# Three attentions with a unit's weighted sums in three parts between the next unit's transposes, and sixteen products ahead of each

## The reference

```python
# layer 0: q = layernorm(x), k = v = ctx, 16 heads of 8
energy = where(mask == 0, -1e20, einsum('nqhd,nkhd->nhqk', q, k))
out = einsum('nhqk,nkhd->nqhd', softmax(energy / sqrt(128)), v)
x = x + (out @ W_out + b_out)
# layer 2: two attention maps over the same values
attn1 = softmax(q1 @ k1.T * SCALE); attn2 = softmax(q2 @ k2.T * SCALE)
y = (attn1 - lambda_full * attn2) @ v1
x = x + (rms_norm(y) * norm_w @ proj_w.T + proj_b)
# layer 3: rotated q and k, a bias by position, a gate over the result
attended = (softmax(q @ k.T * SCALE + bias) @ v) @ Wout.T + b_out
gate = sigmoid(attended @ Wgate.T + b_gate)
x = x + (gate * attended + (1 - gate) * q_input_before_norm)
```

## Time and profile before

| | |
|---|---|
| runs | 1301.16 us median (1288.03 to 1305.8, 3 runs) |
| profiled execution | 1308.73 us, its span 1306.9 us |
| mean granted clock of TensorE | 0.814 |
| busy, share of the span | PE 82%, PEld 75%, DVE 51%, ACT 39%, POOL 30% |
| busy, us | PE 1077.4, DVE 670.0, ACT 513.0, POOL 397.4 |

### The profile page before, as it was taken

The page is one execution under the profiler, slowest core; times in us unless marked ns, Lnnn a source line. Parts: engine busy times, 40 slices in busy tenths (PEclk is TensorE's granted clock), DMA queues, the critical chain, the costliest instruction groups (busy, mean ns, idle before and its releaser), DMA issues. The chain is left out here.

```text
span 1306.9 us, 19893 instructions
## 1 busy us (share of the span) xinstructions
PE 1077.4 (82%) x7374; PEld 976.3 (75%) x7374; DVE 670.0 (51%) x1808; ACT 513.0 (39%) x987; POOL 397.4 (30%) x396
## 2 busy tenths in 40 slices
PE   3899999999988999889989762989169987359992
PEld 2888889999977899768888662888148877358882
DVE  7788511111257343667778643343567655444443
ACT  1443434444433334444444321655224323045552
POOL 4333300010013002300010054446634335545552
PEclk9866589999995899968788765999667656579996
DMA  9999800000000000000000013654200000155553
GB/s 324 170 172 170 156 1 1 1 1 1 1 1 1 1 1 1 1 1 1 1 1 2 1 33 115 177 172 147 65 1 1 1 1 20 36 168 174 174 165 97
DMA packets 70574, 83.52 MB, mean 64 GB/s; under 512 B 5297, under 2 KB 57528, under 8 KB 70352
## 3 DMA queue, kind: packets, MB, share of 16 engines
q1 hardware_dynamic: 64336, 71.71, 24.1%
q0 software_dynamic: 4992, 8.45, 1.9%
q10 hardware_dynamic: 1152, 2.10, 0.4%
HBM read 51.88 MB, written 32.18 MB: 64 GB/s over the span
## 5 line engine op out<-in xcount | busy, mean ns | idle before, releaser
L2167 ACT ACTIVATE hT<-PS,par 128x512 f32<-128x512 f32 x200 | 137.3, 689 | 186.4 <-PE PS L2115 184.9
L2207 DVE SCALAR_TENSOR_TENSOR X<-PS,wts,X 128x128 f32<-128x128 f32 x272 | 76.6, 344 | 231.5 <-PE PS L2127 231.5
L837 PEld LDWEIGHTS PS<-vblk,hT 128*128 128x128 f32 (+1 forms) x1152 | 175.1, 239 | 0.0
L1050 ACT ACTIVATE hT<-PS 128x512 f32<-128x512 f32 (+1 forms) x192 | 91.4, 490 | 205.0 <-PE PS L820 195.3
L837 PE MATMUL PS<-vblk,hT 128*128 128x27 f32 (+2 forms) x1152 | 170.3, 301 | 0.0
L820 PE MATMUL PS<-par,score 128*128 128x128 f32 (+1 forms) x640 | 135.8, 365 | 15.3 <-ACT score L1030 8.1
L820 PEld LDWEIGHTS PS<-par,score 128*128 128x128 f32 (+1 forms) x640 | 106.4, 190 | 25.2 <-issue 13.9
L2127 PEld LDWEIGHTS PS<-regA,hT 128*128 128x128 f32 x1024 | 119.2, 192 | 2.8
L2127 PE MATMUL PS<-regA,hT 128*128 128x128 f32 x1024 | 119.5, 275 | 0.0
L1097 POOL TENSOR_TENSOR score<-score,mx 128x1232 f32<-128x1232 f32 x32 | 72.0, 2249 | 121.7 <-DVE mx L922 121.7
L1878 PE MATMUL PS<-q_up,halves 128*112 128x256 f32 (+1 forms) x276 | 87.9, 318 | 16.1 <-DVE hT L1990 8.8
(11 more groups left out here) (301 smaller groups left out, 2108.9 us busy)
## 6 DMA issues: line engine op xcount, KB each, us to landing
regA<-L3f_w SPq DMA_DIRECT2D x23, 704.0 KB
regB<-L2f_w SPq DMA_DIRECT2D x23, 578.0 KB
L2f_sorted_x<-empty_row SPq DMA_DIRECT2D x8, 1161.0 KB, 21.9
L3f_sorted_x<-empty_row SPq DMA_DIRECT2D x8, 1161.0 KB, 22.1
regA<-L0f_w SPq DMA_DIRECT2D x4, 768.0 KB, 15.9
regA<-L2f_sorted_x SPq DMA_DIRECT2D x23, 129.0 KB, 3.7
regB<-L3f_sorted_x SPq DMA_DIRECT2D x23, 129.0 KB, 4.0
par<-params SPq DMA_DIRECT2D x1, 2386.0 KB, 12.2
```

Of the source, the lines that this page charges most:

```text
L837: last = nc.tensor.matmul(PS[:, 6, h0 * VW:(h0 + nh) * VW], pT, vblk[0:w, b, 3 * j * VW:(3 * j + nh) * VW], start=False, stop=j == NBLK - 1)
L1050: nc.scalar.activation(hT[:, u % 2, i, 0:full], PS[:, bank, 0:full], ACT.Copy)\
L2167: nc.scalar.activation(hT[:, n % 2, k, :], PS[:, i % 4, :], c["act"], bias=pc(f"{tag}_b1")[:, col:col + 1]).then_inc(h_ready.sem, 1)
```

## The change

On TensorE the weighted sums of unit u - 1 are made in iteration u, in three parts that follow the three parts of unit u's transposes; `lag` grows by one. Sixteen products of the identity with itself, which nobody reads, stand between `scores(1)` and the loop. The copies of the turned output (and of the turned attended rows in L3x) go from VectorE to ScalarE. The addition to X (or the gate's) moves into the next unit's `maxima`, between its two operations, and a new signal `att_ready` (after the bias is added) takes the place of `x_done` and `attT` as what the next output transpose waits for. ScalarE copies the first part of a unit's turned blocks before the exponentials of the next unit and the others behind them. Steps of the next norm and of the router start one to three tiles later. The diff, cut to its core:

```diff
-            lag = 1 if tag == "L3x" else 2
+            lag = 2 if tag == "L3x" else 3
...
-                def weighted(u):
+                def weighted(u, i):
                     b = tile_of(u) // TG
-                    if u:
+                    if i == 0 and u:
                         pe.wait_ge(o_used.sem, o_used.at(u))
-                    if tag == "L3x" and u >= 2:
+                    if i == 0 and tag == "L3x" and u >= 2:
                         pe.wait_ge(g_in.sem, g_in.at(u - 1))
-                    for j, (h0, nh, w) in enumerate(BLOCKS):
-                        if j % 4 == 0:
-                            pe.wait_ge(pT_ready.sem, pT_ready.at(3 * u + j // 4 + 1))
+                    pe.wait_ge(pT_ready.sem, pT_ready.at(3 * u + i + 1))
+                    for j in groups[i]:
+                        h0, nh, w = BLOCKS[j]
...
-                        free = aT_ready if tag == "L3x" else x_done
-                        pe.wait_ge(free.sem, free.at(t))
+                        pe.wait_ge(att_ready.sem, att_ready.at(t))
...
                 scores(0)
                 scores(1)
+
+                for _ in range(16):
+                    nc.tensor.matmul(PS[:, 6, 0:P], ident, ident, start=True, stop=True)
                 for u in range(units + lag):
...
                     if 0 < u < units:
-                        transposes(u, (0, 1))
+                        transposes(u, (0,))
+                    if 0 < u <= units:
+                        weighted(u - 1, 0)
+                    if 0 < u < units:
+                        transposes(u, (1,))
                     if done is not None:
                         out_project(done)
+                    if 0 < u <= units:
+                        weighted(u - 1, 1)
...
                     if 0 < u < units:
                         transposes(u, (2,))
+                    if 0 < u <= units:
+                        weighted(u - 1, 2)
...
-                    if u < units:
-                        weighted(u)
...
-                def maxima(u):
+                def maxima(u, between=None):
...
+                    if between:
+                        between()
                     v.wait_ge(scores_used.sem, scores_used.at(u + 1))
                     nc.vector.tensor_reduce(m, dst, AX.X, ALU.max).then_inc(to_shift.sem, 1)
...
                 def finish(t):
                     v.wait_ge(y_psum.sem, y_psum.at(t + 1))
...
+                    att = gdiff[:, t % 2, :] if tag == "L3x" else fin[:, 2 + t % 2, :]
+                    nc.vector.tensor_tensor(att, PS[:, 7, P:2 * P], pc(f"{tag}_bo"), ALU.add).then_inc(att_ready.sem, 1)
+
+                def add_attended(t):
+                    v.wait_ge(att_ready.sem, att_ready.at(t + 1))
+                    nc.vector.tensor_tensor(X[:, t, :], X[:, t, :], fin[:, 2 + t % 2, :], ALU.add).then_inc(x_done.sem, 1)
...
+                    before_last = u - lag - 1
+                    add_to_x = None
+                    if sets == 1 and before_last >= 0:
+                        def add_to_x(t=before_last):
+                            (gate_out if tag == "L3x" else add_attended)(t)
                     if u + 2 < units:
-                        maxima(u + 2)
+                        maxima(u + 2, add_to_x)
...
-                    if u < units:
-                        normalise(u)
+                    if 0 < u <= units:
+                        normalise(u - 1)
...
+                    if done is not None:
+                        evacuate_oT(done)
                     if u < units:
+                        evacuate_pT(u, 0)
                     if u + 1 < units:
                         exps(u + 1)
+                    if tag == "L3x" and done is not None:
+                        evacuate_attT(done)
+                    if u < units:
+                        evacuate_pT(u, 1)
+                        g = route["logits_group"](u) if route else None
+                        if g is not None:
+                            route["scalar_rows"](a, g, bank_of(("rows", g)))
+                        evacuate_pT(u, 2)
...
-            stats_unit = {"L2f": 9, "L3f": 5}[tag]
+            stats_unit = {"L2f": 10, "L3f": 6}[tag]
```

More of the change, by code:

```diff
@@ L745, in attention_stage @@
             x_done = sem("x_done", NT)
+            att_ready = sem("attended", NT)
             if tag == "L3x":
@@ L839, in weighted @@
                                                     start=False, stop=j == NBLK - 1)
-                    last.then_inc(o_psum.sem, 1)
+                    if i == len(groups) - 1:
+                        last.then_inc(o_psum.sem, 1)
                 def out_transpose(t):
@@ new lines, in evacuate_pT @@
+                def evacuate_pT(u, i):
+                    n, width = 3 * u + i, len(groups[i]) * P
+                    bank = bank_of(("exps", n))
+                    a.wait_ge(pT_psum.sem, pT_psum.at(n + 1))
+                    if i == 0 and u >= 2:
+                        a.wait_ge(o_psum.sem, o_psum.at(u - 1))
+                    full = width if groups[i][-1] < NBLK - 1 else width - P
+                    nc.scalar.activation(hT[:, u % 2, i, 0:full], PS[:, bank, 0:full], ACT.Copy)\
+                        .then_inc(*((pT_ready.sem, 1) if full == width else (a_step, st.one())))
+                    if full < width:
+                        rows = BLOCKS[-1][2]
+                        nc.scalar.activation(hT[0:rows, u % 2, i, full:width], PS[0:rows, bank, full:width],
+                                             ACT.Copy).then_inc(pT_ready.sem, 1)
@@ L1033, in scalar @@
                 exps(0)
                 for u in range(units + lag + (tag == "L3x")):
-                    if tag == "L3x" and u >= 2:
-                        t = u - 2
+                    done = after_unit(u) if u < units + lag else None
+                    if tag == "L3x" and u > lag:
+                        t = u - lag - 1
                         a.wait_ge(g_in.sem, g_in.at(t + 1))
                         nc.scalar.activation(gin[:, t % 2, :], gin[:, t % 2, :], ACT.Tanh, scale=0.5).then_inc(g_tanh.sem, 1)
-                    g = route["logits_group"](u) if route else None
+                    if done is not None:
+                        evacuate_oT(done)
@@ L1040, in scalar @@
                     if u < units:
-                        for i, blocks in enumerate(groups):
-                            if i == 2 and g is not None:
-                                route["scalar_rows"](a, g, bank_of(("rows", g)))
-                            n, width = 3 * u + i, len(blocks) * P
-                            bank = bank_of(("exps", n))
-                            a.wait_ge(pT_psum.sem, pT_psum.at(n + 1))
-                            if i == 0 and u >= 2:
-                                a.wait_ge(o_psum.sem, o_psum.at(u - 1))
-                            full = width if blocks[-1] < NBLK - 1 else width - P
-                            nc.scalar.activation(hT[:, u % 2, i, 0:full], PS[:, bank, 0:full], ACT.Copy)\
-                                .then_inc(*((pT_ready.sem, 1) if full == width else (a_step, st.one())))
-                            if full < width:
-                                rows = BLOCKS[-1][2]
-                                nc.scalar.activation(hT[0:rows, u % 2, i, full:width], PS[0:rows, bank, full:width],
-                                                     ACT.Copy).then_inc(pT_ready.sem, 1)
+                        evacuate_pT(u, 0)
@@ L1121, in pool @@
                         route["pool_tile"](p, st, t)
+                if tag == "L0x":
+                    after_nm["pool_group"](p, NG - 2)
                 if tag == "L3x":
-                    for t in range(NT - 3, NT):
+                    for t in range(NT - 4, NT):
                         less_xn(p, t)
```

69 lines of the change are left out of this document (32 added, 37 removed).

## The result

| | before | after |
|---|---|---|
| runs, median | 1297.27 us (1288.03 to 1305.8, 4) | 1376.61 us (1367.61 to 1378.56, 4) |
| ratio | | 1.0599 (1.0546 to 1.0652) |
| profiled span | 1306.9 us | 1374.4 us |
| granted clock, mean | 0.814 | 0.745 |

The change makes the kernel 6% slower. The median before is now of four runs; the prediction had three of them and 1301.16 us. The medians are of all runs and the ratios of the fast ones alone, so that a ratio can lie up to 1% from the quotient of the medians (`fill_L0x`, `turns`, `turns_only` and `each1` have one slow run each).

What follows compares the result with a forecast made beforehand. TensorE was taken to bound the three attentions, half of the time or more at half clock. L2x +42, L0x -1 and L3x -10 us made +31, carried to the median 1332 us; own range 1312 to 1356, wide range 1262 to 1372.

Steps and rivals of the forecast that it cites:

- The sign: Whole kernel: slower, total +31 us; slower by over 2% was given a chance of 0.48.
- The new order keeps either state: TensorE in the attentions: full clock stays if nothing waits; half clock stays until something else, such as router products, lifts it.
- L2x's beginning: Second attention, 32 units: TensorE idles 2.9 us ahead of scores(3), clock falls and stays down; beginning +1 us.
- L2x's sum: Second attention at half clock, 31 units of 7.85 us: 243 us against 201.8, +41; with the beginning +42.
- L0x's beginning: First attention, 16 units: 1.4 us wait ahead of scores(3) probably carried by neighbouring work; beginning -3 us.
- Rival 3: All three attention beginnings fall, the 1.4 us wait being enough: L0x 124 us, kernel 1377 us; chance 0.10.
- The hole of the statistics: L0x at unit 8, L3x after unit 6: weighted sums wait 2.5 to 3 us for the normalisation; clock falls.
- L3x: Third attention, 16 units: 132 us against 135.3, beginning -2, returns of the clock -5; together -10 us.
- VectorE: L0x: the moved addition to X takes 0.3 us, not 2.25; 2 us off VectorE's unit.
- Sixteen products: about 0: Unread products at each attention's beginning: net about 0, bounds -3 and +4 us for each.
- Rival 1: Attentions: clock is held or comes back in an even stream; -119 us, 1182 us; chance 0.10.
- row of 110 to 122: Profile before, L0x: TensorE busy 12.00 of 12 us at clock 0.50, cited against busyness bringing full clock back.

Runs made afterwards that it cites:

- fill_L0x: Changed kernel plus seven unread products between scores(2) and scores(3) of L0x alone; 1350.72 us, 1.0353 of before.
- turns: Changed kernel, waits ahead of scores(3) filled with unread products, first two transpose parts together, then projection and first sums, last transposes, other sums; 1236.49 us, 0.9466 of before.
- turns_only: Changed kernel with the first two transpose parts together and the sums regrouped behind them, waits ahead of scores(3) left unfilled; 1248.2 us, 0.953 of before.
- each1: Changed kernel, waits ahead of scores(3) filled with unread products, plus one unread product ahead of each unit's first transposes; 1244.72 us, 0.9629 of before.
- kick: Changed kernel, waits ahead of scores(3) unfilled, plus one lump of twelve unread products at unit 4 of each attention; 1348.03 us, 1.032 of before.
- kick_again: Changed kernel, waits ahead of scores(3) filled, twelve-product lumps at unit 9 of L0x, 13 and 22 of L2x, 8 and 12 of L3x; 1269.93 us, 0.9703 of before.
- fill_begin: Changed kernel plus unread products between scores(2) and scores(3), 7 in L0x and L3x, 14 in L2x; 1310.13 us, 1.0112 of before.
- lump: Changed kernel with a unit's three parts of weighted sums together again behind the next unit's last transposes; 1290.63 us, 0.9961 of before.

## Why the prediction was wrong in size, and where it was right

The sign was right, and so were the mechanism for half clock and the place of most of the loss; 1332 us was forecast and 1376.6 measured, above the forecast's own range (1312 to 1356) and 4.6 us above the wide one (1262 to 1372). The step that failed is that the beginnings of L0x and L3x carry their hole of 1.4 us (item 4): it was 1.64 us, the clock fell, and in L0x that alone cost 24 us. On the profiled executions it is +31 against +67.5. The 36.5 us between are 19 in L0x (-1 against 20.5 - 2.4), 14 in L2x (+42 against 53.3 + 2.5), 10 in L3x (-10 against 1.5 - 1.8), less 6 outside the attentions, for which nothing was forecast. The other 8 us come from carrying the forecast to a median that was 7.6 us below the profiled execution before and is not after.

1. *"The new order keeps either state."* Right for half clock: 232 us in L2x, 137 in L0x, though TensorE was busy for 248.12 of 255.12 and 120.23 of 120.62 us. For full clock the forecast's condition, "if nothing waits", was needed: in `kick` the level held for eight plain units with their short waits, in `kick_again` one such wait of 0.53 us ended it.
2. *L2x's beginning.* Right: a hole of 2.9 us was forecast, 3.12 measured, the clock down right behind, units of 7.3 us without output and 8.0 with, 7.65 on average (forecast 7.85).
3. *L2x's sum.* 243 us forecast, 255.1 measured. The terms that were mis-sized: the products of the router were left out, 2.5 us for each of three groups (9.87 us where a unit without output takes 7.33) and 4 for the ranks, +11; the full clock behind the ranks lasted 3.4 us and not three units, +5; units shorter, -6; the stop of 5.25 us for the choice as forecast, two others of 0.87 us, +2. Together +12.
4. *L0x's beginning.* Here the step failed: "1.4 us, which the products and T(0) on one side and S, T0, W0 on the other probably carry". The hole measured 1.64 us, TensorE was busy 1.76 of the 3.4 us around it, and the clock was gone: 120.62 us where 102 was forecast, and `fill_L0x` puts 24 us on this one hole. Rival 3 had it: 124 us for L0x, 1377 for the kernel, at a chance of 0.10. The nearest row was at hand: in the earlier trace rows the clock fell behind a stretch in which TensorE was busy 3.18 of 3.3 us. A hole of 1.4 us is worse than that stretch, and the prediction gave no row in which such a hole was carried. L3x has the same hole and fell too (item 6).
5. *The hole of the statistics.* With the beginning filled the clock fell at unit 8 in L0x, as forecast, and at the router's statistics in L2x and L3x. But the cause in L0x was one step earlier: statistics of 0.86, 0.38 and 0.93 us ahead of the normalisation made 1.29 us, and `apply`, to which the forecast put a hole of 2.5 to 3 us, came after the fall. Its length was foreseen (3.06 us against 2.0 + 1.1), but TensorE waited only 0.75 us for the normalisation behind it. For L2x see `kick`: the router's narrow products may have their part.
6. *L3x.* Forecast -10, measured about 0 (+1.5 and -1.8): the beginning fell here too, at 1046.5, which the forecast had not counted, and with it filled the stage took 117.90 us (`fill_begin`) and not 136.80. The clock came back at 1080.7 and 1131.9, as forecast for the stage with more products behind the output.
7. *VectorE.* The addition to X takes 0.28 us and not 2.25, as forecast, and no time was won by it (`lump`); that this is because TensorE bounds the stage is argued from its busy share, not shown.
8. *Sixteen products: about 0.* Right, in either order.
9. *Rival 1* (the clock is held) is what `each1`, `kick` and `turns` come near to. "Continuously busy" is not what does it: 12.00 of 12 us busy at 0.50, 11.20 of 12 at 1.00. By the Trainium skill ("TensorE: Matmul & The Clock Gate", Loop structure matters more than you think) products that follow each other without a wait keep the engine at full clock; the 30 us from 610 in `kick`, 27.38 of them busy at 1.00, agree. That staying busy also brings the full clock back, the rule that the prediction set against its row of 110 to 122, fails again in the changed kernel. The Trainium skill (the same page, Part 4: PE-mode transpose) says that the full clock doesn't engage for products in transpose mode; in `turns` the rise of 574.2 stands behind eight transposes with projection and wide sum, and no run here shows whether the transposes run in that mode. The rival's "about once in 24 us" was misread, too: the clock of the kernel before rose eleven times in the 201.8 us of L2x.

## What to carry to other kernels

When TensorE's granted clock goes to and fro, look for what lifts it as well as for what drops it: here mixing wide work (transposes, 128 columns) and narrow work (sums of 18 or 27 columns) evenly took away both, and then a short wait could cost the rest of the stage. Try one lump of wide work in each period (here eight transposes side by side), with which most falls lasted less than a unit, and look first at the stage's beginning, where pipelines are not yet filled. Price a hole by how long the lower level lasts behind it, not by its own length.

## What the runs showed of the hardware

- One order of instructions ran at either level for a long time: 124 passes in 12 us at 1.00 and 72 at 0.50 in one stage of one run (`fill_begin`). At the lower level TensorE was the busier (12.00 against 11.47 us).
- Idle time of 1.64 us was enough for a fall to 0.50 that then lasted 137 us; 0.53 us was enough once (`kick_again`, 590.4) and not in other units; 1.02 us was followed by a fall 2.3 us later in `fill_begin` (613.4) and 4.6 us later in `kick` (643.9).
- About 5 us of 128-column products (24 passes) brought the clock back before they had ended, and it stayed for 37 us (`kick`).
- On VectorE, `apply` of the earlier trace rows, 1.10 us for four, took 3.06 us where it began 0.04 us behind GpSimd's shift of 2.25 us (`fill_begin`, 74.71) and 1.77 where it began 0.92 us before the shift's end (the changed kernel, 97.66): in both some 0.85 us were left behind that end; the statistics' small operation on 4 columns took 0.93 us beside the shift and 0.17 without it. The Trainium skill ("SBUF — State Buffer", Who interferes with whom) has VectorE and GpSimd share a pair of ports that one of them takes for a whole instruction; the rows agree with it.
